# The start of a two-layer conditional residual kernel rewritten: loads on two queues, a shorter sort, and eight multiplications by zeros on TensorE

## The chip, the cores and the metric

The kernel runs on one core of a Trainium2 chip. The metric is the device time of one execution in microseconds (us). A profile is one further execution, recorded by the hardware profiler. Engines are named as the profile names them: PE is TensorE's matmul, PEld its weight load, DVE is VectorE, ACT is ScalarE, POOL is GpSimd, SP is the engine that only issues transfers. "SPq" and "ACTq" are the two engines' issuing of DMA transfers.

## What is computed

The input `x` is 128 batches of 64 channels by 512. Each batch `b` has a subject (0 to 7) and an adapter (0 to 6).

```
x  = x + einsum('bct,bcd->bdt', x, weights[subject]) + bias[subject][:, :, None]
H  = einsum('btd,od->bto', x, W)                       # W is 512 x 512
xa = einsum('btd,brd->btr', x, A[adapter])             # rank 16
x  = x + H + einsum('btr,bor->bto', xa, Bm[adapter]) * scalings[adapter]
```

Everything is fp32.

## The kernel before, in words

**Sorting.** Batches are sorted by adapter on the chip, so that two batches with the same adapter form a pair; a pair fills 128 partitions (two times 64 channels). 64 pairs are then processed in sorted order. The sort is made of two small matmuls that count adapters (L657, L658: `counts` and `earlier`), a chain of small DVE operations (L415 to L462), and three matmuls that turn `place` into tables (L680, L682). It gives three things: `order`, the adapters in the order in which they come (semaphore `order_ready`), `batch`, the sorted batch numbers (`batches_ready`), and `table` with subjects and adapter places (`others_ready`).

**Merged weights.** For each adapter in that order the kernel makes one matrix, W transposed plus the adapter's product, in four chunks of 128 by 512 (`m_product` L692, one matmul a chunk), kept as a high and a low part for fp32r matmuls: `m_add` (DVE) adds the product in PSUM to the transposed weight `wt`, `m_round` (ACT) makes `m_hi`, `m_split` (DVE) makes `m_lo`. The operands `a_parts` and `b_parts` are made the same way: the load `a_f` and the transposed `b_dup` (`turn_b`, four transposes L674) are each rounded by ACT and split by DVE. W arrives in `w_nat` (printed as o_ring, whose memory it shares) and is turned by TensorE in column blocks, `turn_w(c)` L664, and copied out by ACT, `copy_wt`.

**Pairs.** `layer0(j)` is 32 small matmuls (L716) on the pair's slot of `x_ring` (four slots) with `p_pair`, which POOL places with `bias_pair`. `x1_add` (DVE), `x1_round` (ACT), `x1_split` (DVE) follow, then `layer1(j)`, 12 matmuls of 128 by 512 (L739), then `copy_out` (ACT) and two stores. In the steady part TensorE does four `layer0` in a row every four pairs.

**Order by hand.** Every engine's program is written out; only semaphores tie them. SP issues, in order: the adapter numbers, `b_nat`, `p_all` twice, W blocks 0 and 1; then it waits for `order_ready` and issues `load_a(0)`, W block 2, the bias, W block 3; then it waits for `batches_ready` and issues eight loads of x (four pairs, `x_first`), `load_a(1)`, and `load_quad(4)`: the loads of pairs 4 to 7, each of which waits until `layer0` has freed its slot, in slot order 0, 2, 1, 3. ACT issues the scalings (spread over 128 partitions) and the subjects. On TensorE, before the first `layer1`, stand `layer0(0)`, `layer0(1)` and `turn_b(1)`; `layer0(2)` and `layer0(3)` stand between `layer1(0)` and `layer1(1)`, and `layer0` of pairs 4, 6, 5, 7 between `layer1(1)` and `layer1(2)`.

Of the kernel before, what the change touches and what calls it, by code (L numbers as in the profile page):

```python
# [33 lines left out]
def cond_residual_layers(nc, x, subject, bias, adapter, w, W, A, Bm, scal, out):  # L34
# [25 lines left out]
    with ExitStack() as ctx:  # L60
# [34 lines left out]
        scal_all = sb("scal_all", [P, K])  # L95
        neg = sb("neg", [P, 2])
# [4 lines left out]
        ids = sb("ids", [P, 2])  # L101
        vals = sb("vals", [P, 3], BF16)
        onehot = sb("onehot", [P, K], BF16)
        cnt_i = sb("cnt_i", [P, 2, K], I32)
        even_odd = sb("even_odd", [P, 2, K])
        key = sb("key", [P, K])
        prec = sb("prec", [P, K, K])
        prec_n = sb("prec_n", [P, 2, K, K])
        at_place = sb("at_place", [P, K, K])
        start = sb("start", [P, 2, K])  # L110
        last = sb("last", [P, K])
        quant = sb("quant", [P, 3, K])
        quant_b = sb("quant_b", [P, 3])
        small = sb("small", [P, 2])
# [5 lines left out]
        order_f = sb("order_f", [1, K])  # L120
# [4 lines left out]
        b_turned_at = ps[:, 4, :].rearrange("p (c n) -> p n c", c=TC)  # L125
# [19 lines left out]
        scal_in = sem("scal_in")  # L145
        consts = sem("consts")
# [5 lines left out]
        place_ready = sem("place_ready")  # L152
        batches_tabled = sem("batches_tabled")
# [6 lines left out]
        b_nat_ready = sem("b_nat_ready")  # L160
# [70 lines left out]
        def _(sp):  # L231
            with nc.allow_non_contiguous_dma(reason="indices, one per partition"):
                sp.dma_start(ids_i[:, 0:1], adapter.rearrange("(b a) -> b a", a=1)).then_inc(ids_in, 16)
            sp.dma_start(b_nat[:], Bm.rearrange("k (p c) r -> p k (c r)", c=TC)).then_inc(bnat_in, 16)
            for half in range(2):
                sp.dma_start(p_all[C * half:C * half + C], w.rearrange("s c d -> c s d")).then_inc(w0_in, 16)

            def load_w(c):

                cols = slice(c * P, c * P + P)  # L240
                sp.dma_start(w_nat[:, :, cols], W[:, cols].rearrange("(o p) t -> p o t", p=P)).then_inc(w_in[c], 16)

            load_w(0)
            load_w(1)
# [24 lines left out]
            load_w(2)  # L269
            sp.dma_start(bias_all[:], bias.rearrange("s d -> (s d)").rearrange("(a n) -> a n", a=1)  # L270
                         .to_broadcast([P, S * C]).rearrange("p (s d) -> p s d", s=S)).then_inc(bias_in, 16)
            load_w(3)
# [26 lines left out]
        def _(pool):  # L299
# [31 lines left out]
            pool.wait_ge(scal_in, 16)  # L331
            nc.gpsimd.tensor_tensor(b_nat[:], b_nat[:], scal_all[:].unsqueeze(2).to_broadcast([P, K, TC * R]),
                                    ALU.mult).then_inc(b_nat_ready, 1)
            pool.wait_ge(b_nat_ready, 1)
            regs = [pool.alloc_register(f"pool_word{i}") for i in range(2)]

            def dup_b(i):
                k, = words(pool, regs[:1], order[0:1, ds(i, 1)], K - 1)

                at_least(pool, b_turned, i)  # L340
                nc.gpsimd.tensor_copy(b_dup[:, :, 0:G, :], b_nat[:, ds(k, 1), :].rearrange("p k (c r) -> p (k c) r", c=TC)  # L341
                                      .unsqueeze(2).to_broadcast([P, TC, G, R])).then_inc(b_dupped, 1)
# [41 lines left out]
        def _(dve):  # L384
# [11 lines left out]
            def tt(o, a, b, op):  # L396
# [3 lines left out]
            over_k = [P, K, K]  # L400

            dve.wait_ge(consts, 2)
            iota_done = did(nc.vector.tensor_copy(iota[:], iota_i[:]))

# [6 lines left out]
            need(did(nc.vector.tensor_copy(ids[:, 0:1], ids_i[:, 0:1])))  # L411
            nc.vector.tensor_scalar(onehot[:], iota[:, 0:K], ids[:, 0:1], None, ALU.is_equal).then_inc(oh_ready, 1)
# [4 lines left out]
            cnt_done = did(nc.vector.tensor_copy(cnt_i[:, 0], counts))  # L417
            need(key_done)
            prec_done = tt(prec[:], key[:].unsqueeze(1).to_broadcast(over_k), key[:].unsqueeze(2).to_broadcast(over_k),
                           ALU.is_gt)  # L420
            need(cnt_done)
            odd_done = did(nc.vector.tensor_scalar(cnt_i[:, 1], cnt_i[:, 0], 1, None, ALU.bitwise_and))
            need(prec_done)
            place_of_done = did(nc.vector.tensor_reduce(quant[:, 1, :], prec[:], AX_X, ALU.add))
            need(odd_done)
            did(nc.vector.tensor_copy(even_odd[:, 1], cnt_i[:, 1]))
            even_done = tt(even_odd[:, 0], counts, cnt_i[:, 1], ALU.subtract)

            need(place_of_done)
            at_done = tt(at_place[:], quant[:, 1, :].unsqueeze(1).to_broadcast(over_k),  # L430
                         iota[:, 0:K].unsqueeze(2).to_broadcast(over_k), ALU.is_equal)
            need(even_done)

            prec_n_done = [tt(prec_n[:, h], prec[:], even_odd[:, h].unsqueeze(1).to_broadcast(over_k), ALU.mult)
                           for h in range(2)][-1]
            need(at_done)
            at_done = tt(at_place[:], at_place[:], iota[:, 0:K].unsqueeze(1).to_broadcast(over_k), ALU.mult)
            need(prec_n_done)
            start_done = did(nc.vector.tensor_reduce(start[:].rearrange("p h k -> p (h k)"),
                                                     prec_n[:].rearrange("p h k m -> p (h k) m"), AX_X, ALU.add))  # L440
            need(at_done)
            order_done = did(nc.vector.tensor_reduce(order_f[:], at_place[0:1], AX_X, ALU.add))
            need(start_done)

            tt(quant[:, 0, :], start[:, 0], earlier, ALU.add)
            left_done = tt(start[:, 1], start[:, 1], start[:, 0], ALU.subtract)
            need(order_done)
            nc.vector.tensor_copy(order[:], order_f[:]).then_inc(order_ready, 1)
            whole_done = did(nc.vector.tensor_reduce(small[:, 0:1], even_odd[:, 0], AX_X, ALU.add))
            last_done = tt(last[:], even_odd[:, 0], earlier, ALU.is_equal)  # L450
            did(nc.vector.tensor_copy(vals[:, 0:1], pid_i[:]))
            need(whole_done)
            need(did(nc.vector.scalar_tensor_tensor(out=start[:, 1], in0=start[:, 1], scalar=small[:, 0:1],
                                                    in1=even_odd[:, 0], op0=ALU.add, op1=ALU.subtract)))
            need(tt(quant[:, 2, :], last[:], start[:, 1], ALU.mult))

            need(tt(quant[:], quant[:], onehot[:].unsqueeze(1).to_broadcast([P, 3, K]), ALU.mult))
            dve.wait_ge(subject_in, 16)
            did(nc.vector.tensor_copy(vals[:, 1:2], ids_i[:, 1:2]))
            need(did(nc.vector.tensor_reduce(quant_b[:], quant[:], AX_X, ALU.add)))  # L460
# [19 lines left out]
            def m_add(t, chunk):  # L480

                dve.wait_ge(m_summed, t + 1)
                if isinstance(t, int) and t < TC:
                    dve.wait_ge(wt_copied, t + 1)
# [26 lines left out]
            b_split(0)  # L511
            a_split(0)
            m_add(0, 0)
            m_add(1, 1)
            m_split(0, 0)
            m_split(1, 1)
            m_add(2, 2)
# [301 lines left out]
```

## Time and profile before

| | us |
|---|---|
| median of three runs | 262.65 (261.12 to 262.7) |
| the profiled execution | 263.65 |
| its span, first to last instruction | 261.6 |
| PE busy | 237.2 (91%) |
| DVE, ACT, POOL busy | 142.9, 112.5, 75.9 |
| mean granted TensorE clock | 0.984 |

The profiled execution takes 2.05 us more than its span. The profile gives busy times, a line of the granted clock in 40 slices (each 6.54 us), the chain of waits that ended last, and groups of instructions; the timeline gives each instruction's start and duration.

### The profile page before, as it was taken

The numbers are of one execution on the slowest core, as the hardware profiler recorded it, in microseconds if no ns is written. First come the engines' busy times: TensorE is split into PE (matmuls) and PEld (weight loads), VectorE is DVE, ScalarE is ACT, GpSimd is POOL, SyncE is SP. The second block draws the span as 40 slices with busy tenths as digits, with TensorE's granted clock in tenths as the row PEclk, the third lists the DMA queues.
The fourth block names the chain that finished last, engine by engine and source line by source line (L and its number), as shares of the span: only waits on it lengthen the run. The fifth ranks groups of instructions, "written<-read, shape, count | busy, mean of one in ns | idle before, by whom it ended". The sixth has DMA issues, their size and how long they took to land.

```text
span 261.6 us, 9840 instructions
## 1 busy us (share of the span) xinstructions
PE 237.2 (91%) x2929; PEld 195.0 (75%) x2930; DVE 142.9 (55%) x242; ACT 112.5 (43%) x189; POOL 75.9 (29%) x284
## 2 busy tenths in 40 slices
PE   0487498999999999999999999999999998999993
PEld 0465386788887888788878887888878886888882
DVE  5669436747476564747474647556574744343300
ACT  2164405535354436444353535353634443343511
POOL 6346520045103530154005510355342423000000
PEclk9999859999999999999999999999999999999998
DMA  6582535255554656365536465456547362642331
GB/s 114 152 197 63 164 106 178 61 159 153 164 167 127 180 145 196 86 199 135 180 100 191 139 165 165 119 169 160 175 101 210 104 198 76 201 125 78 83 76 45
DMA packets 25825, 36.68 MB, mean 140 GB/s; under 512 B 6736, under 2 KB 8784, under 8 KB 25808
## 3 DMA queue, kind: packets, MB, share of 16 engines
q1 hardware_dynamic: 20400, 28.06, 39.8%
q10 hardware_dynamic: 5408, 8.40, 11.0%
q8 instruction: 10, 0.16, 0.3%
q14 instruction: 7, 0.06, 0.1%
HBM read 19.67 MB, written 16.78 MB: 139 GB/s over the span
## 4 chain that ended last, share of the span: by engine, by line
PE 84%; DMA 4%; DVE 4%; issue 3%; ACT 2%; SPq 1%; ACTq 0%
PE ps L739 68%; PE ps L716 13%; PE ps L692 3%; DMA a_f<-in_L_cond_A_dram 2%; SPq L256 1%; DVE m_f L486 1%; PE ps L674 1%; DMA x_ring<-in_x_dram 1%; DMA ids_i<-in_itok_B_dram 1%; ACT x_hi L576 1%; DVE m_lo L492 1%; DVE prec_n L397 0%; ACTq L602 0%; PE ps L664 0%; DVE x_lo L506 0%
## 5 line engine op out<-in xcount | busy, mean ns | idle before, releaser
L739 PE MATMUL ps<-m_hi,x_hi 128*128 x264 | 105.9, 401 | 3.0 <-DVE x_lo L506 1.8
L739 PE MATMUL ps<-m_hi,x_lo 128*128 x264 | 103.2, 391 | 0.0
L739 PE MATMUL ps<-m_lo,x_hi 128*128 x264 | 103.2, 391 | 0.0
L506 DVE TENSOR_TENSOR x_lo<-x,x_hi 128x512 fp32r<-128x512 f32 x64 | 44.5, 695 | 81.6 <-ACT x_hi L576 81.5
L368 POOL COPY p_pair<-p_all 64x64 f32 x128 | 41.8, 327 | 102.5 <-issue 54.8
L576 ACT ACTIVATE x_hi<-x 128x512 fp32r<-128x512 f32 x64 | 40.4, 632 | 50.0 <-DVE x L498 31.9
L585 ACT ACTIVATE o_ring<-ps 128x512 f32<-128x512 f32 x60 | 35.8, 596 | 60.3 <-PE ps L739 60.1
L739 PEld LDWEIGHTS ps<-m_hi,x_hi 128*128 128x128 f32 x264 | 49.8, 189 | 14.5 <-issue 3.6
L739 PEld LDWEIGHTS ps<-m_hi,x_lo 128*128 128x128 f32 x264 | 49.7, 188 | 10.8
L739 PEld LDWEIGHTS ps<-m_lo,x_hi 128*128 128x128 f32 x264 | 49.9, 189 | 9.7
L498 DVE TENSOR_TENSOR x<-ps,bias_pair 128x512 f32<-128x512 f32 x64 | 43.7, 683 | 10.7 <-PE ps L716 10.7
L716 PEld LDWEIGHTS ps<-p_pair,x_ring 64*64 64x64 f32 x2048 | 33.3, 140 | 11.8 <-issue 11.7
L716 PE MATMUL ps<-p_pair,x_ring 64*64 64x64 f32 x2048 | 35.6, 225 | 5.4 <-DMA x_ring<-in_x_dram 3.3
L379 POOL COPY bias_pair<-bias_all 128x64 f32 x128 | 28.4, 248 | 2.7 <-DMA bias_all<-in_fside_8xS_dram 2.4
L570 ACT ACTIVATE m_hi<-m_f 128x512 f32 (+1 forms) x32 | 20.1, 631 | 16.0 <-DVE m_f L486 16.0
L486 DVE TENSOR_TENSOR m_f<-ps,wt 128x512 f32<-128x512 f32 x32 | 21.8, 688 | 5.6 <-PE ps L692 4.0
L492 DVE TENSOR_TENSOR m_lo<-m_f,m_hi 128x512 f32 (+1 forms) x32 | 22.6, 705 | 0.7 <-ACT m_hi L570 0.5
L341 POOL COPY b_dup<-b_nat 128x256 f32 x8 | 3.6, 445 | 36.4 <-PE ps L674 34.6
L692 PE MATMUL ps<-b_parts,a_parts 128*128 128x512 f32 x32 | 12.8, 416 | 1.0 <-DVE a_parts L471 1.0
L692 PEld LDWEIGHTS ps<-b_parts,a_parts 128*128 128x128 f32 x32 | 6.2, 202 | 2.6 <-DVE a_parts L471 1.4
L477 DVE SCALAR_TENSOR_TENSOR b_parts<-b_parts,neg,ps 128x512 fp32r<-128x512 f32 x8 | 5.9, 735 | 1.7 <-ACT b_parts L565 1.7
L587 ACT ACTIVATE o_ring<-ps 64x512 f32<-64x512 f32 x4 | 2.4, 591 | 9.3 <-PE ps L739 9.3
(79 smaller groups left out, 57.1 us busy)
## 6 DMA issues: line engine op xcount, KB each, us to landing
x_ring<-in_x_dram SPq DMA_DIRECT2D x128, 128.0 KB, 2.7
out_dram<-o_ring ACTq DMA_DIRECT2D x64, 128.0 KB, 2.4
out_dram<-o_ring SPq DMA_DIRECT2D x64, 128.0 KB, 2.3
o_ring<-in_L_cond_W_dram SPq DMA_DIRECT2D x4, 256.0 KB, 4.5
a_f<-in_L_cond_A_dram SPq DMA_DIRECT2D x8, 128.0 KB
b_nat<-in_L_cond_Bm_dram SPq DMA_DIRECT2D x1, 256.0 KB, 4.2
p_all<-in_L_cond_weights_dram SPq DMA_DIRECT2D x2, 128.0 KB, 4.3
bias_all<-in_fside_8xS_dram SPq DMA_DIRECT2D x1, 256.0 KB, 5.3
```

Of the source, the lines that this page charges most:

```text
L368: nc.gpsimd.tensor_copy(p_pair[rows, slot, :], p_all[rows, ds(s[half], 1), :] .rearrange("p s d -> p (s d)")).then_inc(pair_ready, 1)
L379: nc.gpsimd.tensor_copy(bias_pair[:, slot, C * half:C * half + C], bias_all[:, ds(s[half], 1), :] .rearrange("p s d -> p (s d)")).then_inc ...
L486: nc.vector.tensor_tensor(m_f[:, chunk % 2], ps[:, 4 + chunk % 2, :], wt[:, chunk, :], ALU.add).then_inc(m_added, 1)
L492: nc.vector.tensor_tensor(m_lo[:, cols], m_f[:, chunk % 2], m_hi[:, cols], ALU.subtract).then_inc(m_ready, 1)
L498: nc.vector.tensor_tensor(x1[:, u % 2].rearrange("p c (h d) -> p c h d", h=2), l0_out(u).rearrange("p h (c d) -> p c h d", c=TC), bias_pai ...
L506: nc.vector.tensor_tensor(x1_lo[:, u % HELD], x1[:, u % 2], x1_hi[:, u % HELD], ALU.subtract).then_inc(x1_lo_ready, 1)
L570: nc.scalar.activation(m_hi[:, cols], m_f[:, chunk % 2], ACT.Copy).then_inc(m_hi_ready, 1)
L576: nc.scalar.activation(x1_hi[:, u % HELD], x1[:, u % 2], ACT.Copy).then_inc(x1_hi_ready, 1)
L585: nc.scalar.activation(o_ring[:, u % OR, :], ps[:, 2 + u % 2, :], ACT.Copy).then_inc(out_ready, 1)
L692: nc.tensor.matmul(ps[:, 4 + chunk % 2, :], a_parts[:, chunk * P:chunk * P + P], b_parts[:], start=True, stop=True).then_inc(m_summed, 1)
L716: mm = nc.tensor.matmul(x1_t[side * C:side * C + C, half, c * C:c * C + C], x_ring[rows, slot, at:at + C], p_pair[rows, u % PR, :], start= ...
L739: mm = nc.tensor.matmul(ps[:, bank, :], part[:, u % HELD, c, :], m[:, ds(k * (TC * T) + c * T, T)], start=(c == 0 and part is x1_hi and m ...
```

## The change

It does six things, nearly all before the first `layer1`.

1. **Loads.** SP issues the adapter numbers, W row blocks 0 and 1 (whole rows of 2 KB, where columns of 512 B were loaded), the subjects and one row of scalings (`scal_row`, 32 B). ACT issues `b_nat`, W row blocks 2 and 3, `p_all` twice and the bias. After `order_ready` SP issues only `load_a(0)`.
2. **Scalings.** A matmul of ones with `scal_row` spreads them; ACT copies them to `scal_all`. POOL no longer multiplies all of `b_nat`; each `dup_b` is a multiplication of its 128 by 256 block instead of a copy.
3. **Sort.** Most DVE steps work on 128 by 8 with an accumulated output in place of 128 by 64. `order` comes from a new matmul of `vals` with `firsts`, copied out by ACT, in place of a DVE reduction.
4. **Zeros.** TensorE multiplies `b_parts`, set to zero by a DVE memset, by itself (128 by 512, bf16): five times at its start, three times between the scalings' matmul and the order's.
5. **First merged matrix.** W is turned by row block into four PSUM banks, copied from there (two chunks by ACT, two by DVE), and the products of the first adapter are accumulated onto it in PSUM, so that `m_round_first` and `m_split_first` read PSUM and the first four `m_add` are gone.
6. **First pairs.** `layer0` of pairs 0 to 3 all stand before `layer1(0)`, `turn_b(1)` before `layer1(1)`, and the first `load_quad` takes its slots in the order 0, 1, 2, 3.

The core of the diff, engine by engine. On SP:

```diff
+            for o in range(2):
+                sp.dma_start(w_nat[:, o, :], W[o * P:o * P + P, :]).then_inc(w_in[o], 16)
+            with nc.allow_non_contiguous_dma(reason="indices, one per partition"):
+                sp.dma_start(ids_i[:, 1:2], subject.rearrange("(b a) -> b a", a=1)).then_inc(subject_in, 16)
+            sp.dma_start(scal_row[:], scal.rearrange("(a k) -> a k", a=1)).then_inc(scal_in, 16)
...
-                for i in (0, 2, 1, 3):
-                    sp.wait_ge(l0_done, i + 1 if isinstance(j, int) and j == XR else j - XR + (1, 3, 2, 4)[i])
+                first = isinstance(j, int) and j == XR
+                for i in range(L0_QUAD) if first else (0, 2, 1, 3):
+                    sp.wait_ge(l0_done, i + 1 if first else j - XR + (1, 3, 2, 4)[i])
...
             sp.wait_ge(order_ready, 1)
             load_a(0)
-            load_w(2)
-            sp.dma_start(bias_all[:], bias.rearrange("s d -> (s d)").rearrange("(a n) -> a n", a=1)
...
-            load_w(3)
```

On DVE:

```diff
+            nc.vector.memset(b_parts[:].bitcast(F32), 0.0).then_inc(zeroed, 1)
...
+            nc.vector.scalar_tensor_tensor(out=firsts[:], in0=iota[:, 0:K], scalar=place_of,
+                                           in1=was_first.to_broadcast([P, K]),
+                                           op0=ALU.is_equal, op1=ALU.mult).then_inc(firsts_ready, 1)
...
+            copy_wt(2)
+            copy_wt(3)
+            m_split_first(0)
             x1_add(0, 0)
-            m_split(2, 2)
+            m_split_first(1)
+            x1_add(1, 1)
             x1_split(0, 0)
```

On ACT:

```diff
+            act.wait_ge(scal_spread, 1)
+            nc.scalar.activation(scal_all[:], ps[:, 6, 0:K], ACT.Copy).then_inc(scal_ready, 1)
...
+            act.wait_ge(order_summed, 1)
+            nc.scalar.activation(order[:], ps[0:1, 7, 0:K], ACT.Copy).then_inc(order_ready, 1)
```

On TensorE:

```diff
+            pe.wait_ge(zeroed, 1)
+            keep_busy(5)
...
             nc.tensor.matmul(ps[:, 0, K:2 * K], before_b[:], onehot[:], start=True, stop=True).then_inc(counted, 1)
...
+            pe.wait_ge(scal_in, 16)
+            nc.tensor.matmul(ps[:, 6, 0:K], ones[0:1, :], scal_row[:], start=True, stop=True).then_inc(scal_spread, 1)
...
+            keep_busy(3)
+            pe.wait_ge(firsts_ready, 1)
+            nc.tensor.matmul(ps[0:1, 7, 0:K], vals[:, 3:4], firsts[:], start=True, stop=True).then_inc(order_summed, 1)
+            turn_w(0)
             pe.wait_ge(place_ready, 1)
```

How the rows on TensorE stand from its start to the products of the first adapter. Before (a row is the line, the operation, output and inputs, the shape, and what it waits for):

```order
L657 MATMUL ps<-onehot,ones_b 128x8 [waits oh_ready,consts_b]
L658 MATMUL ps<-onehot,before_b 128x8
L680 MATMUL ps<-place,vals 1x128 [waits place_ready]
L682 MATMUL ps<-place,vals 1x128 x2
L674 MATMUL ps<-ident,b_dup 128x128 [waits b_dupped]
L674 MATMUL ps<-ident,b_dup 128x128 x3
L664 MATMUL ps<-ident,o_ring 128x128 [waits w_in0]
```

The same place on TensorE after the change, where ps<-b_parts are the zeros, ps<-firsts the order and ps<-place the tables:

```order
L684 MATMUL ps<-b_parts 128x512 [waits zeroed]
L684 MATMUL ps<-b_parts 128x512 x4
L692 MATMUL ps<-onehot,ones_b 128x8 [waits oh_ready,consts,consts_b]
L693 MATMUL ps<-onehot,before_b 128x8
L695 MATMUL ps<-scal_row,ones 128x8 [waits scal_in]
L684 MATMUL ps<-b_parts 128x512 x3
L721 MATMUL ps<-firsts,vals 1x8 [waits firsts_ready]
L701 MATMUL ps<-ident,o_ring 128x128 [waits w_in0]
L701 MATMUL ps<-ident,o_ring 128x128 x3
L724 MATMUL ps<-place,vals 1x128 [waits place_ready]
L727 MATMUL ps<-place,vals 1x128 [waits order_ready]
```

Between the counts and the tables now stand the wait for the scalings' transfer, three multiplications of zeros, the order's matmul and the turning of one row block of W.

TensorE from the first pair's `layer0` to the first `layer1` (L739 before). Before:

```order
L716 MATMUL ps<-p_pair,x_ring 64x64 [waits pair_ready,x_first0,others_ready]
L716 MATMUL ps<-p_pair,x_ring 64x64 x15
L716 MATMUL ps<-p_pair,x_ring 64x64 [waits pair_ready,x_first1]
L716 MATMUL ps<-p_pair,x_ring 64x64 x15
L674 MATMUL ps<-ident,b_dup 128x128 [waits m_added,b_dupped]
L674 MATMUL ps<-ident,b_dup 128x128 x3
L221 TENSOR_LOAD table
L739 ISA [waits m_ready,x1_lo_ready]
```

And after the change, where `layer1` is L794:

```order
L773 MATMUL ps<-p_pair,x_ring 64x64 [waits pair_ready,x_first0]
L773 MATMUL ps<-p_pair,x_ring 64x64 x15
L743 MATMUL ps<-b_parts,a_parts 128x512 [waits wt_copied_too]
L773 MATMUL ps<-p_pair,x_ring 64x64 [waits pair_ready,x_first1,others_ready]
L773 MATMUL ps<-p_pair,x_ring 64x64 x15
L773 MATMUL ps<-p_pair,x_ring 64x64 [waits x1_ready,pair_ready,x_first2]
L773 MATMUL ps<-p_pair,x_ring 64x64 x15
L773 MATMUL ps<-p_pair,x_ring 64x64 [waits x1_ready,pair_ready,x_first3]
L773 MATMUL ps<-p_pair,x_ring 64x64 x15
L228 TENSOR_LOAD table
L794 ISA [waits m_ready,x1_lo_ready]
```

The third and fourth pair's `layer0` and their waits for x moved ahead of the first `layer1`, and `turn_b(1)` moved behind it.

## Rows read from the trace of the kernel before

**Rows 1.** The page: the granted clock in 40 slices, in tenths.

```profile
PEclk9999859999999999999999999999999999999998
```

**Rows 2.** Windows, PE: stretch, length, PE busy (instructions), granted clock, DMA share, GB/s.

```profile
60.00:240.00 180.00, 177.05 (x2324) 1.00 0.53 150
```

**Rows 3.** Timeline, the sort: start, duration, engine, line, operation, [idle before <-releaser].

```profile
4.53 0.17 PE L657 MATMUL ps<-onehot,ones_b 128*128 128x8 bf16 x1 [4.53 <-DVE onehot L412]
...
5.64 1.20 DVE L397 TENSOR_TENSOR prec_n<-prec,even_odd 128x64 f32<-128x64 f32 x2
...
7.36 0.15 DVE L448 CAST order<-order_f 1x8 int32<-1x8 f32 x1
...
8.24 0.70 SPq L251 DMA_DIRECT2D a_f<-in_L_cond_A_dram  x1
...
10.35 0.28 DVE L466 CAST batch<-ps 1x128 int32<-1x128 f32 x1 [0.36 <-PE ps L680]
...
11.81 2.54 SPq L256 DMA_DIRECT2D x_ring<-in_x_dram  x4
```

**Rows 4.** DMA issues: what, by whom, how many, size, median us to landing.

```profile
x_ring<-in_x_dram SPq DMA_DIRECT2D x128, 128.0 KB, 2.7
...
o_ring<-in_L_cond_W_dram SPq DMA_DIRECT2D x4, 256.0 KB, 4.5
...
b_nat<-in_L_cond_Bm_dram SPq DMA_DIRECT2D x1, 256.0 KB, 4.2
...
ids_i<-in_itok_B_dram ACTq DMA_DIRECT2D x1, 0.5 KB, 3.3
```

**Rows 5.** Chain of work that ended last, in order of time: start, duration, what.

```profile
8.24 4.79 DMA a_f<-in_L_cond_A_dram
...
21.97 3.02 PE ps L739 x12
...
29.32 2.77 DMA x_ring<-in_x_dram
...
32.57 3.69 PE ps L716 x128
36.27 3.84 PE ps L739 x12
```

**Rows 6.** Timeline, from the turning of B to the first m_f.

```profile
10.46 1.11 PE L674 MATMUL ps<-ident,b_dup 128*128 128x128 f32 x4
...
13.06 0.63 ACT L559 ACTIVATE a_parts<-a_f 64x512 fp32r<-64x512 f32 x1 [0.85 <-DMA a_f<-in_L_cond_A_dram]
...
13.72 0.74 DVE L471 SCALAR_TENSOR_TENSOR a_parts<-a_parts,neg,a_f 64x512 fp32r<-64x512 f32 x1 [0.66 <-ACT a_parts L559]
...
15.35 1.29 DVE L486 TENSOR_TENSOR m_f<-ps,wt 128x512 f32<-128x512 f32 x2 [0.89 <-PE ps L692]
...
19.51 0.66 PE L674 MATMUL ps<-ident,b_dup 128*128 128x128 f32 x4
```

**Rows 7.** Waits: who for whom, us in total, times, longest.

```profile
SPq L256 <- PE ps L716: 4.9, 1, 4.9
```

**Rows 8.** Windows of layer0 (L716) alone: PE busy, PEld busy, granted clock, DMA, GB/s.

```profile
32.00:37.00 5.00, 3.69 (x128) 3.54 (x128) 0.50 0.39 97
50.00:54.00 4.00, 2.10 (x128) 1.99 (x128) 1.00 0.43 108
```

**Rows 9.** Windows of layer1 (L739) alone, same columns.

```profile
26.00:28.85 2.85, 2.83 (x12) 2.17 (x12) 1.00 0.42 109
```

**Rows 10.** Windows, all engines: PE, PEld, DVE, ACT, POOL busy, granted clock, DMA, GB/s.

```profile
28.90:32.50 3.60, 0.36 (x2) 0.00 (x0) 1.29 (x2) 1.40 (x3) 2.00 (x11) 0.84 0.71 212
30.90:37.70 6.80, 5.13 (x132) 4.75 (x133) 1.99 (x3) 0.81 (x2) 2.45 (x12) 0.53 0.38 99
```

**Rows 11.** The page's groups: POOL's copies for the pairs | busy, mean ns | idle before.

```profile
L368 POOL COPY p_pair<-p_all 64x64 f32 x128 | 41.8, 327 | 102.5 <-issue 54.8
...
L379 POOL COPY bias_pair<-bias_all 128x64 f32 x128 | 28.4, 248 | 2.7 <-DMA bias_all<-in_fside_8xS_dram 2.4
```

More of the change, by code:

```diff
@@ L100, in cond_residual_layers @@
         ids_i = sb("ids_i", [P, 2], I32)
-        ids = sb("ids", [P, 2])
-        vals = sb("vals", [P, 3], BF16)
+        vals = sb("vals", [P, 4], BF16)
+        firsts = sb("firsts", [P, K], BF16)
         onehot = sb("onehot", [P, K], BF16)
         cnt_i = sb("cnt_i", [P, 2, K], I32)
-        even_odd = sb("even_odd", [P, 2, K])
+        even = sb("even", [P, K])
         key = sb("key", [P, K])
[L107 to L114, printed above, removed]
+        picked = sb("picked", [P, 4, K])
+        own = sb("own", [P, 12])
         place = sb("place", [P, B], BF16)
@@ L436, in _ @@
[L436 to L457, printed above, removed]
+            need(own_done)
+            place_done = did(nc.vector.tensor_scalar(picked[:, 2], key[:], own_key, None, ALU.is_gt, ALU.add,
+                                                     accum_out=place_of))
@@ L465, in _ @@
+            nc.vector.tensor_scalar(place[:], iota[:], at, None, ALU.is_equal).then_inc(place_ready, 1)
             dve.wait_ge(batches_tabled, 1)
@@ L653, in _, with keep_busy @@
         def _(pe):
+            zeros = b_parts[:].bitcast(BF16)
+            def keep_busy(times):
+                for _ in range(times):
+                    nc.tensor.matmul(ps[:, 3, :], zeros[:, 0:P], zeros[:, 0:T], start=True, stop=True)
+            pe.wait_ge(zeroed, 1)
+            keep_busy(5)
             pe.wait_ge(consts_b, 3)
+            pe.wait_ge(consts, 3)
             pe.wait_ge(oh_ready, 1)
@@ L685, in _, with m_product_first @@
             turn_b(0)
-            turn_w(0)
-            turn_w(1)
+            for o in range(1, TC):
+                turn_w(o)
+            for c in range(TC):
+                nc.tensor.matmul(ps[:, FIRST + c, c * P:c * P + P], ident_b[:], ident_b[:],
+                                 start=False, stop=True).then_inc(wt_turned, 1)
+            def m_product_first(chunk):
+                if chunk < 2:
+                    pe.wait_ge(wt_copied, chunk + 1)
+                else:
+                    pe.wait_ge(wt_copied_too, chunk - 1)
+                nc.tensor.matmul(ps[:, FIRST + chunk, :], a_parts[:, chunk * P:chunk * P + P], b_parts[:],
+                                 start=False, stop=True, skip_group_check=True).then_inc(m_summed, 1)
             def m_product(t, chunk):
-                at_least(pe, m_added, t - 1)
+                at_least(pe, m_added, t - TC - 1)
                 nc.tensor.matmul(ps[:, 4 + chunk % 2, :], a_parts[:, chunk * P:chunk * P + P], b_parts[:],
@@ L748, in _ @@
             pe.wait_ge(b_ready, 1)
[L749 to L755 removed]
+            m_product_first(0)
+            m_product_first(1)
+            m_product_first(2)
             first_inputs(0)
             layer0(0, 0)
[L758 to L760 removed]
+            m_product_first(3)
+            pe.wait_ge(others_ready, 2)
+            for j in range(1, L0_QUAD):
+                first_inputs(j)
+                layer0(j, j)
             regs = [pe.alloc_register(f"pe_word{i}") for i in range(2)]
@@ L775, in step @@
                     turn_b(n + 2)
+                if n is None and j == 1:
+                    turn_b(1)
                 if n is not None and u == HEAD + 2:
```

202 lines of the change are left out of this document (109 added, 93 removed).

## The prediction, made before the changed kernel ran

> **What bounds the kernel now.** I read the page first, then windows, then the chain in order of time, then the timeline of the first 40 us. The page's line of the granted clock dips in the fifth and sixth slice [rows 1]. From 60 to 240 us PE is busy 177.05 of 180 us [rows 2]: there TensorE is the bound, and what is done before it starts moves the end one for one. The change leaves the steady part as it is, so the question is only how early the steady part begins.
>
> The chain of the start has four pieces to keep in mind. The load of A is issued at 8.24 us and takes 4.79 us to land, the first `layer1` starts at 21.97 us, a load of x is waited for until 32.1 us, and then `layer0` and `layer1` of the next pairs take 3.69 and 3.84 us [rows 5]. The load of x is late because its issue is: SP waited 4.9 us for a `layer0` [rows 7]. That is `layer0(2)`, which stands behind `layer1(0)`, and the loads for pairs 5 to 7 stand behind that wait. PE is then nearly idle from 28.9 to 32.5 us (0.36 us busy of 3.6), and the granted clock is 0.53 over 30.9 to 37.7 us [rows 10], that is the 1.2 GHz level for nearly all of that stretch.
>
> The page shows a granted clock of full speed at the very start, but the instructions say otherwise: four transposes take 1.11 us at 10.46 us and 0.66 us at 19.51 us [rows 6]. I read TensorE as at its lower level until about 17 us.
>
> **The change part by part.**
>
> *When the order is ready.* Before, counts are out at 4.7 us and `order` is copied by DVE at 7.36 to 7.51 us [rows 3]. DVE's new chain is shorter: of about 19 small steps up to `order` the two `prec_n` alone took 1.20 us [rows 3] and are gone; about ten steps of some 0.12 us remain, so `firsts` is ready near 6.0 us. But the order now also needs TensorE, which first waits for the scalings. Their transfer is SP's fifth. I put its issue near 2.7 us, from four issues of about 0.46 us ahead of it after 0.85 us. Its landing is bounded from below by the 3.3 us of a transfer of 0.5 KB that had its queue almost to itself, and from above by the 4.5 us of a W block that stood behind others [rows 4]: 6.0 to 7.2 us. I take 6.0, by the row of its own size. Then come its matmul (0.2 us), three multiplications of zeros, the order's matmul (0.2) and ACT's copy (0.27). One 128 by 512 matmul takes 2.83/12 = 0.24 us at 2.4 GHz [rows 9], so three take 0.7 us, or 1.4 at the lower level. That gives 7.4 to 8.1 us; I take 8.0, so 0.5 us later than now. The load of A is issued 0.73 us after the order, at 8.75 us.
>
> A rule bears on this wait. The trace shows that the 0.5 KB of subjects landed in 3.3 us while `b_nat`, issued at nearly the same time on the other queue, took 4.2 us [rows 4]: the small transfer was not held by the large one. The Trainium skill (DMA: Bandwidth & Descriptors, "Queues, rings and completion order") says that a transfer's semaphore increment lands only after every earlier write of that DMA engine, across its queues. By the page the scalings would be held by W's first two blocks and `b_nat` too, and the order would be ready near 9.2 us, 1.2 us later than I take; this case is a rival below, by the 4.5 us row.
>
> *The load of A.* It no longer shares its queue with W blocks 2 and 3 and the bias. A load of x of the same 128 KB takes 2.7 us [rows 4], so it lands at 11.5 us, where it was 13.03. ACT's rounding and DVE's split take 0.63 and 0.74 us [rows 6]: `a_parts` is ready at 12.9 us, where it was 14.46.
>
> *From A to the first `layer1` on DVE.* After `a_parts` DVE has two copies of W, then two splits, two `x1_add` and one `x1_split`: seven operations of 128 by 512, which run at one each 0.62 us when nothing is waited for (two in 1.29 us, rows 6 show it). So `x1_lo` of pair 0 is ready at 12.9 + 7 x 0.63 = 17.3 us. The two remaining splits of M end before `layer1(0)` reaches its third and fourth chunk.
>
> *The first four x loads.* All four `layer0` now stand ahead of `layer1(0)`. TensorE turns one block of W after the order (1.06 us at the low level, as four transposes of 1.11 us [rows 6] show), then makes the batch table. So `batch` is copied near 9.4 us, where it was 10.35 to 10.63 [rows 3]. SP's first x load follows 1.2 us later (11.81 after 10.63 [rows 3]), at 10.7 us. Four issues take 2.54 us [rows 3], so the eighth starts at 15.2 and lands 2.7 us later, at 17.9 us. `layer0(3)` takes 2.10/4 = 0.5 us [rows 8], and `layer1(0)` starts at 18.4 us. That is later than DVE's 17.3, so **this path decides: 21.97 - 18.4 = 3.6 us gained.** DVE's `place`, some ten small steps behind `firsts`, is ready near 7.3 us and hidden behind the order's wait.
>
> *From there to the second group of pairs.* Now it is 32.57 - 21.97 = 10.6 us. After: two `layer1` of 2.83 us [rows 9], `turn_b(1)` 0.66 [rows 6], one product 0.24, together 6.55 us, to 24.95 us. The x loads for it: SP has issued the first eight by 15.8, `load_a(1)` by 16.5, and eight more from 17.0; the last starts at 21.5 and lands at 24.2 to 24.5 us, just hidden by `layer1(1)`. If that cover is gone, each 0.1 us of lateness costs 0.1. **Gained: 10.6 - 6.55 = 4.05 us.**
>
> *The lower level of the clock.* `layer0` of four pairs took 3.69 us at it and takes 2.10 at full clock [rows 8]; the 12 matmuls behind took 3.84 [rows 5] against 2.83 [rows 9]. If the idle stretch is gone I expect the low stretch gone: **1.6 + 1.0 = 2.6 us.**
>
> *Costed at nothing.* The five zeros need 5 x 0.48 = 2.4 us at the low level and run while TensorE waits for the one-hot at 4.53 us [rows 3]. DVE's memset runs while it waits for iota. The multiplication in `dup_b` is off the path: POOL has slack. A pair takes it two copies of 0.33 us and two of 0.25 [rows 11], 1.15 us and, with the gaps between, some 1.5; eight pairs from 10.4 us end near 22.5 us, ahead of the 24.95 where they are needed. If that cover is gone, POOL's lateness adds to the start of the second group one for one.
>
> Sum: 3.6 + 4.05 + 2.6 = 10.2 us. Against the profiled execution of 263.65 us that is 253.4; the median of the runs shown is 1.0 us lower, so I expect 252.4 us.
>
> **The rivals.**
>
> *A, the clock falls anyway (25%, 255 us).* Between 12.9 and 18.4 us TensorE has only three products and four `layer0`, some 3 us of work in 5.5, waiting on x. Before, a stretch with 0.36 us of work in 3.6 was followed by 6.8 us at the lower level [rows 10], which cost 2.6 us. If the same comes here, over `layer1(0)`, most of the third term is given back: 252.4 + 2.6 = 255.0. Against it: the stretch is fuller than the one that brought the fall, and the zeros keep the engine active early. The Trainium skill (TensorE: Matmul & The Clock Gate, Part 1) says the low clock is the default, sustained activity releases it and idleness brings it back; it would have the zeros work and the gaps behind them undo it.
>
> *B, the scalings are late (15%, 253.6 us).* They land at 7.2 instead of 6.0 us, the bound of [rows 4]; order, batch and A all slip by 1.2 us.
>
> *C, better (15%, 250.8 us).* The zeros bring 2.4 GHz before 6 us: three zeros save 0.7 us, the block of W 0.4 us, and A and x come 1.1 us earlier; x loads closer to 2.4 us give the rest.
>
> *D, x still waited for (5%, 257 us).* If the second eight loads of x or POOL's pairs land 4 to 5 us later than worked out, the 3.6 us stall and with it the low clock return, and only the first term and a little are left: 259 us at worst.
>
> *E, slower (2%, above 264 us).* The lower level lasts. Four `layer0` cost 1.6 us more and 12 matmuls 1.0 us more at it, so each `layer1` at the low level loses about 1 us of 3.8. To eat 10.2 us it must hold over the first ten pairs, nearly 40 us. The longest low stretch before PE's last work is 6.8 us [rows 10]; nothing speaks for it but that the start has more waits.
>
> *F, the zeros do nothing.* The first stretch stays at 1.2 GHz until about 17 us as before. My sum already has the low level there, so the time is that of the forecast; they cost nothing either.
>
> **How the numbers follow.** The forecast as worked out has 38%, with F in it. A, B, C, D and E have 25, 15, 15, 5 and 2%. A and B together would give 256.2; C at its best 249.5. The range 249.5 to 256.3 leaves out D, E and tails of A and C, together under 2 in 10. About 1% is what a measurement can tell from no change, here 2.6 us. Faster by over 1% (under 260.0): 0.95; within 1%: 0.03; slower: 0.02.
>
> **What would show it.** `layer1(0)` starts near 18.4 us and waits last for x or for `layer0(3)`; the wait of 4.9 us on SP is gone; the second group's `layer0` starts near 25 us; the granted clock has no low stretch in the slices after the first; four transposes of B take 0.66 us if C is right and 1.1 if not; the scalings' matmul is near 6.0 us. Wrong would be: a low clock over the first `layer1` (A), the order's matmul above 8.5 us (B), PE waiting for DMA before the second group (D).

## The result: no gain, where 4% was forecast

The changed kernel took 264.6 us (median of 20 runs, 263.47 to 266.49); the kernel before, in 20 runs, 263.27 us (261.12 to 266.44). The ratio is 1.0066, with a 95% interval of 1.004 to 1.0091: slower by 0.7%. I had forecast 252.4 us. The trace below is of an execution of 266.09 us, at a mean granted clock of 0.971; the 20 runs had 0.971 to 0.994, and the five from 0.993 up took 263.5 to 264.6 us, so the stretches of low clock that the trace shows were shorter in some executions.

The profile after. The page's span and granted clock in 40 slices:

```profile
span 264.4 us, 9858 instructions
...
PEclk9977959999999999999999999999999999999998
```

The span is 2.8 us longer than before, and the clock line has two dips where [rows 1] has one. The chain that ended last, in order of time (start, duration, what):

```profile
2.74 5.18 DMA scal_row<-in_L_cond_scalings_dram
...
8.55 1.39 PE ps L684 x3
...
10.96 4.97 DMA a_f<-in_L_cond_A_dram
...
24.02 3.03 PE ps L794 x12
...
30.47 5.00 issue
35.46 3.69 PE ps L773 x128
39.16 3.67 PE ps L794 x12
...
47.82 5.48 PE ps L794 x24
```

Against [rows 5]: the first `layer1` starts at 24.02 us, where it was 21.97 and I had put 18.4; A takes 4.97 us to land, where I had put 2.7; and there is again an idle stretch, 5.00 us long, before the second group's `layer0`, which starts at 35.46 us instead of the 24.95 I expected. Behind it `layer0` takes 3.69 us, the same number as in [rows 5]: the low clock came back with the stall. The steady part starts 2.7 us late (the last line; before, a like block started at 45.11 us), and the span grew by 2.8.

SP's timeline (start, duration, engine, line, what), and POOL's waits (who, for whom, us in total, times, longest):

```profile
20.97 5.12 SPq L257 DMA_DIRECT2D x_ring<-in_x_dram  x8
```

```profile
POOL b_dup L336 <- PE ps L714: 7.0, 1, 7.0
POOL b_dup L336 <- ACT order L635: 6.7, 1, 6.7
```

The loads of x are not what is late: SP issued the second group's eight without a pause from 20.97 to 26.1 us, and a load of x took 2.4 to 3.0 us to land, so the last was in by 29.1 us, ahead of the stall. The first POOL line names what I had missed (the second is `dup_b(0)`, which waits for the order). POOL's timeline around it, and TensorE's transposes that it waits for:

```profile
20.30 0.41 POOL L377 COPY bias_pair<-bias_all 128x64 f32 x2
...
27.70 0.61 POOL L336 TENSOR_TENSOR b_dup<-b_nat,scal_all 128x256 f32 x1 [6.99 <-PE ps L714]
...
29.30 0.30 POOL L366 COPY p_pair<-p_all 64x64 f32 x1 [0.99 <-POOL b_dup L336]
...
34.50 0.41 POOL L377 COPY bias_pair<-bias_all 128x64 f32 x2
```

```profile
26.89 0.60 PE L714 MATMUL ps<-ident,b_dup 128*128 128x128 f32 x4
```

POOL has placed pairs 0 to 3 by 20.7 us. Next in its program is `dup_b` of the third adapter, ahead of pair 4. It may not overwrite `b_dup` until `turn_b(1)` has read it, and the change moved `turn_b(1)` from before `layer1(0)` (19.51 us, [rows 6]) to behind it (ending at 27.5 us). Pairs 4 to 7 are placed only then, from 29.30 to 34.91 us (the last POOL line is pair 7's), and TensorE's `layer0` of the group, which needs all four, starts at 35.46 us. The page calls TensorE's 5.00 us "issue", since it waits on a count that POOL raised piece by piece.

### The profile page after: what moved, and what is told of

It is laid out like the page before. It is cut to its first block, busy times and chain, and to the rows that moved or that the text cites. A ratio compares the mean times of both kernels' runs of the same rounds, so it can differ in the third digit from the quotient of the medians.

```text
span 264.4 us, 9858 instructions
## 1 busy us (share of the span) xinstructions
PE 242.2 (92%) x2940; PEld 196.9 (74%) x2941; DVE 138.8 (53%) x242; ACT 111.5 (42%) x189; POOL 75.5 (29%) x283
## 4 chain that ended last, share of the span: by engine, by line
PE 86%; issue 4%; DMA 4%; DVE 2%; ACT 1%; SPq 1%; ACTq 0%
PE ps L794 68%; PE ps L773 13%; PE ps L749 2%; DMA scal_row<-in_L_cond_scalings_dram 2%; DMA a_f<-in_L_cond_A_dram 2%; PE ps L714 1%; PE ps L743 1%; DVE m_f L484 1%; DVE m_lo L490 1%; PE ps L684 1%; ACT x_hi L600 0%; ACTq L626 0%; SPq L242 0%; DVE a_parts L471 0%; DVE x L508 0%
## 5 line engine op out<-in xcount | busy, mean ns | idle before, releaser
L794 PE MATMUL ps<-m_hi,x_hi 128*128 x264 | 105.7, 400 | 1.3 <-DVE m_lo L490 1.2
L794 PE MATMUL ps<-m_hi,x_lo 128*128 x264 | 103.3, 391 | 0.0
L794 PE MATMUL ps<-m_lo,x_hi 128*128 x264 | 103.1, 391 | 0.0
L794 PEld LDWEIGHTS ps<-m_hi,x_hi 128*128 128x128 f32 x264 | 49.8, 189 | 12.8 <-issue 1.9
L794 PEld LDWEIGHTS ps<-m_hi,x_lo 128*128 128x128 f32 x264 | 49.7, 188 | 10.7
L794 PEld LDWEIGHTS ps<-m_lo,x_hi 128*128 128x128 f32 x264 | 49.8, 189 | 9.7
L773 PEld LDWEIGHTS ps<-p_pair,x_ring 64*64 64x64 f32 x2048 | 34.8, 145 | 14.1 <-issue 14.1
L773 PE MATMUL ps<-p_pair,x_ring 64*64 64x64 f32 x2048 | 37.1, 231 | 7.2 <-issue 7.2
L594 ACT ACTIVATE m_hi<-m_f 128x512 f32 (+1 forms) x28 | 17.7, 632 | 13.1 <-DVE m_f L484 13.1
L484 DVE TENSOR_TENSOR m_f<-ps,wt 128x512 f32<-128x512 f32 x28 | 19.2, 690 | 5.4 <-PE ps L749 3.8
L490 DVE TENSOR_TENSOR m_lo<-m_f,m_hi 128x512 f32 (+1 forms) x28 | 19.7, 703 | 0.1
L336 POOL TENSOR_TENSOR b_dup<-b_nat,scal_all 128x256 f32 x8 | 5.2, 652 | 44.6 <-PE ps L714 37.6
L749 PE MATMUL ps<-b_parts,a_parts 128*128 128x512 f32 x28 | 10.7, 389 | 0.0
L471 DVE SCALAR_TENSOR_TENSOR a_parts<-a_parts,neg,a_f 64x512 fp32r<-64x512 f32 x8 | 5.9, 738 | 2.2 <-ACT a_parts L576 2.2
L714 PE MATMUL ps<-ident,b_dup 128*128 128x128 f32 x32 | 5.4, 294 | 1.2 <-DVE m_f L484 0.9
```

What stands on the lines that cost most here:

```text
L484: nc.vector.tensor_tensor(m_f[:, chunk % 2], ps[:, 4 + chunk % 2, :], wt[:, chunk, :], ALU.add).then_inc(m_added, 1)
L490: nc.vector.tensor_tensor(m_lo[:, cols], m_f[:, chunk % 2], m_hi[:, cols], ALU.subtract).then_inc(m_ready, 1)
L594: nc.scalar.activation(m_hi[:, cols], m_f[:, chunk % 2], ACT.Copy).then_inc(m_hi_ready, 1)
L749: nc.tensor.matmul(ps[:, 4 + chunk % 2, :], a_parts[:, chunk * P:chunk * P + P], b_parts[:], start=True, stop=True).then_inc(m_summed, 1)
L773: mm = nc.tensor.matmul(x1_t[side * C:side * C + C, half, c * C:c * C + C], x_ring[rows, slot, at:at + C], p_pair[rows, u % PR, :], start= ...
L794: mm = nc.tensor.matmul(ps[:, bank, :], part[:, u % HELD, c, :], m[:, ds(k * (TC * T) + c * T, T)], start=(c == 0 and part is x1_hi and m ...
```

## The experiments

All times below stand against runs of the kernel before on the same chip (263.04, 263.04, 263.08 and 262.87 us in the four groups).

### POOL's order

`pool_dup_later`, one edit of the changed kernel:

```diff
-                place_at = n + 2 if n is not None and u == HEAD else 1 if n is None and j == 1 else None
+                place_at = n + 2 if n is not None and u == 0 else 1 if n is None and j == 1 else None
```

> The changed kernel with one edit: POOL makes each later dup_b (those of the third adapter on) after it has placed the pairs of the group, not before. Theory P (POOL's dup_b of the third adapter waits for turn_b(1), which the change moved behind layer1(0); pairs 4 to 7 are placed only after it, so TensorE idles 5.0 us from 30.5 to 35.5 us and its clock falls): the idle 5.0 us and most of the low clock behind it (3.69 for 2.10 us of layer0, some 1 us of layer1) go, the time falls by 6 to 7.6 us against the changed kernel, to 257 to 258.5 us. Rival X (the loads of x for pairs 4 to 7 are what is waited for, as I forecast could happen): the time stays within 1 us of 264.6.

Measured: 258.26 us, ratio 0.9842 (0.9774 to 0.991), below the changed kernel by 6.3 us in the medians and 5.9 in the ratios. Its chain:

```profile
23.10 3.01 PE ps L794 x12
...
26.55 2.77 PE ps L794 x12
...
29.55 2.02 PE ps L773 x128
```

The stall is gone and `layer0` takes 2.02 us. Theory P is shown; theory X falls. One line of POOL's program, which the change had left as it was, had turned a gain of 1.6% into a loss, because TensorE's `turn_b(1)` had moved.

### The part of the change by itself

`before_layer0_ahead` is the kernel before with `layer0(2)` and `layer0(3)` moved ahead of `layer1(0)` and the first `load_quad` in the order 0 to 3:

```diff
             layer0(1, 1)
             turn_b(1)
+            for j in range(2, L0_QUAD):
+                first_inputs(j)
+                layer0(j, j)
```

> The kernel before with one part of the change alone: layer0 of pairs 2 and 3 ahead of layer1(0), the first load_quad in the order 0 to 3; turn_b(1) stays ahead of both. My prediction's second and third term by themselves: layer1(0) starts about 1 us later (23 us, layer0(3) waits for x1_add(1)), the wait for x at 29 to 32.6 us goes, so the second group's layer0 starts near 29 us instead of 32.57, and the low clock (2.6 us) goes: 263 - 3.5 - 2.6 = 257 us. Rival: if POOL's pairs or the loads still come late, 261 us or more.

Measured: 258.84 us, ratio 0.9845 (0.9788 to 0.9902). Its chain:

```profile
23.27 5.75 PE ps L738 x24
...
29.24 0.82 issue
30.06 2.09 PE ps L717 x128
```

The wait for x and the low clock over the second group are gone. So my second and third term were real. From `layer1(0)` to the second group it is 6.8 us, where it was 10.6 (3.8 us gained, 4.05 forecast), and `layer0` and `layer1` behind take 2.09 and 2.94 us, where they took 3.69 and 3.84 (2.5 gained, 2.6 forecast). Against that, `layer1(0)` starts 1.3 us later (23.27 against 21.97). That leaves 5.0 us, as in the spans (256.6 against 261.6); the medians differ by 4.2. With its own `turn_b(1)` in place, POOL does not stall here. Moving `layer0` thus gives 1.6% alone; all the other edits of the change together, with POOL's order mended, give nothing beyond it (0.9842 against 0.9845).

### The small transfers and the zeros

`small_first` issues the scalings and the subjects ahead of W's two blocks on SP.

```diff
+            sp.dma_start(scal_row[:], scal.rearrange("(a k) -> a k", a=1)).then_inc(scal_in, 16)
             with nc.allow_non_contiguous_dma(reason="indices, one per partition"):
                 sp.dma_start(ids_i[:, 1:2], subject.rearrange("(b a) -> b a", a=1)).then_inc(subject_in, 16)
+            for o in range(2):
+                sp.dma_start(w_nat[:, o, :], W[o * P:o * P + P, :]).then_inc(w_in[o], 16)
-            sp.dma_start(scal_row[:], scal.rearrange("(a k) -> a k", a=1)).then_inc(scal_in, 16)
```

> The changed kernel with one edit: on SP the scalings and the subjects are issued ahead of the two row blocks of W. Theory S (the 32 B of scalings land 5.2 us after their issue because they stand behind W's blocks on SP's queue): they land near 1.33 + 3 = 4.3 us instead of 7.9, the order comes near 6.4 us instead of 10.25, layer1(0) starts about 3 us earlier than 24.0. But the stall by POOL stays, whose chain (turn_b(1), dup_b, four pairs placed) starts from layer1(0), so the gain is 3 to 3.8 us: 261 us. Rival L (small transfers take 5 us whenever large ones of either queue are in flight): the order stays near 10 us and the time at 264.6.

Measured: 263.62 us, ratio 1.0019 (0.998 to 1.0057). Its timeline:

```profile
4.08 0.59 PE L695 MATMUL ps<-scal_row,ones 1*128 1x8 f32 x2
...
6.56 0.15 ACT L635 ACTIVATE order<-ps 1x8 int32<-1x8 f32 x1
...
8.68 1.12 PE L701 MATMUL ps<-ident,o_ring 128*128 128x128 f32 x4 [2.51 <-DMA o_ring<-in_L_cond_W_dram]
```

Theory S holds for the order: 6.56 us instead of 10.08. But the time fell by about 1 us (the intervals of the two ratios meet), not by 3 to 3.8: TensorE now waits 2.51 us for W's first block, which stands ahead of the tables, so the batch numbers come at 10.0 us, and the pairs' placing is late. And the clock takes part of the gain. The window in which TensorE waits for the pairs (columns as below, under `fill_the_wait`), and `layer1(0)` on the chain:

```profile
17.00:20.00 3.00, 1.39 (x64) 1.17 (x64) 2.40 (x5) 1.75 (x3) 1.57 (x9) 1.00 0.32 87
```

```profile
21.79 3.99 PE ps L794 x12
```

`layer1(0)` starts 2.2 us earlier than in the changed kernel, but takes 3.99 us instead of 3.03: after 3 us with 1.39 of work the granted clock is 0.50 from 20.5 to 23.8 us. That is my rival A as I had put it.

`no_zeros` leaves out both calls of `keep_busy`.

> The changed kernel without its eight multiplications of zeros. Theory N (the zeros raise no clock, and the three ahead of the order stand on the chain for 1.4 us): order 1.4 us earlier, time 1 to 1.5 us lower, 263.3 us, and the granted clock of the first 13 us unchanged at the lower level. Rival W (the zeros do keep the clock up for part of the start): the time rises by 1 us or more.

Measured: 263.18 us, ratio 1.0031 (0.9995 to 1.0067); the order is out at 8.61 us, 1.47 earlier. That is 1.4 us below the changed kernel by the medians and 0.9 by the ratios, whose intervals meet, so the price on the end is likely and not shown. The batch numbers gain less than the order, 0.64 us (10.68 against 11.32): they also need the subjects, which took 7.1 us to land (issued at 2.26, behind W's two blocks). `pool_and_small` joins the first two edits, `pool_small_no_zeros` takes the zeros from that.

> The changed kernel with both edits: POOL's later dup_b behind the group's pairs, and the scalings and subjects ahead of W. If both theories hold and their gains add: 264.6 - 7 - 3.5 = 254 us. If the second group's x loads are now what is waited for, up to 1.5 us of that is lost, 255.5 us. If the x loads and not POOL bound it, 260 us or more.

> The changed kernel with POOL's dup_b later, the small transfers first, and none of the eight zeros. With the small transfers first, the three zeros end (6.07 us) near the moment firsts is ready, and W's first block, which lands near 8.6 us, holds the tables anyway. Theory N (zeros change nothing but the chain they stand on): the order comes some 0.4 us earlier, the time stays within 0.7 us of 257.65. Rival W (the zeros hold the clock): it rises by 1 us or more.

Measured: 257.65 us, ratio 0.9823 (0.9755 to 0.9892), and 257.49 us, ratio 0.977 (0.9705 to 0.9835). The gains did not add to 254: W's block and the pairs bind, as in `small_first`, and the clock falls over `layer1(0)` in both traces (3.94 and 5.41 us for its 12 matmuls). The zeros make no difference that can be told here.

`tables_first_no_zeros` moves `turn_w(0)` behind the tables and `turn_b(0)`.

```diff
-            turn_w(0)
             pe.wait_ge(place_ready, 1)
...
-            for o in range(1, TC):
+            for o in range(TC):
```

> As the last, and TensorE makes the tables before it turns W's first block. Theory T (in the last kernels the tables wait for W's block, 2.5 us): batch is copied near 7.3 us instead of 10.0, x loads start near 8.7 instead of 11.5, the pairs are placed 2 us earlier, and layer1(0) starts near 19 us instead of 21.2; time 255.3 us. Rival A (the load of A with its 5 us is now what decides): A lands at 12.3 us as now, layer1(0) near 20 us, time 256.5 us.

Measured: 255.69 us, ratio 0.9737 (0.9672 to 0.9802). The batch numbers come at 7.1 us, `layer1(0)` at 20.93, and what stands right ahead of it is `layer0(3)`, which waited for POOL's placing of pair 3. `layer1(0)` takes 3.02 us: here the clock did not fall, though TensorE had as little work ahead of it (1.31 us of the 3 from 17 to 20 us) as in `small_first`. What decides between the two, no run shows. Theory T's time is met, its start of `layer1(0)` is 2 us too early. `pairs_earlier` adds two edits for POOL: `dup_b(1)` after the first four pairs, and `p_all` issued ahead of W's blocks 2 and 3.

> tables_first_no_zeros with two edits for POOL: dup_b(1) after the first four pairs, and ACT issues p_all ahead of W's blocks 2 and 3. There layer1(0) starts at 20.93 us right behind layer0(3) (19.93), which waited for POOL's pair 3; DVE's x1_split(0) was done at 18.9. Theory: layer1(0) moves to DVE's 18.9 to 19.3 us, time 255.7 - 1.8 = 253.9 us. Rival: the loads of x for the second group (issued one by one behind x_first and load_a(1)) then bind, gain under 0.5 us.

Measured: 253.76 us, ratio 0.9653 (0.9604 to 0.9702). Its chain:

```profile
18.00 3.01 PE ps L794 x12
...
24.59 2.09 PE ps L773 x128
...
34.65 5.47 PE ps L794 x24
```

These are about the times that I had forecast for the change itself (18.4 and 24.95 us), but it took six edits more to get there, and A's load still takes 4.39 us, not the 2.7 forecast. It has the lowest median of the versions that compute the whole result, 3.5% below the kernel before; `pairs_earlier_zeros` and `all_together` below can't be told from it.

`pairs_earlier_zeros` puts the eight zeros back into it.

> pairs_earlier with the eight zeros put back in their places. Theory N: they stand on the order's chain for some 0.3 us (small transfers first, three zeros end near 6.0 us) and raise no clock: the granted clock reaches 2.4 GHz near 13 us as without them, time within 0.8 us of 253.76. Rival W: the clock comes up by 8 us, the transposes of B and W take 0.66 us in place of 1.1, and the time falls by over 0.5 us.

Measured: 254.39 us, ratio 0.9689 (0.9638 to 0.974). Its transposes of B behind the zeros, and the same four in `pairs_earlier` without zeros:

```profile
4.60 1.46 PE L687 MATMUL ps<-b_parts 128*128 128x512 bf16 x3
...
7.88 1.11 PE L717 MATMUL ps<-ident,b_dup 128*128 128x128 f32 x4 [0.59 <-POOL b_dup L336]
```

```profile
7.72 1.12 PE L716 MATMUL ps<-ident,b_dup 128*128 128x128 f32 x4 [0.42 <-POOL b_dup L336]
```

1.11 and 1.12 us are both the lower level (0.66 at the higher, [rows 6]). Five zeros in 2.3 us and three in 1.5 us raised nothing that reached the next work. Nor did they bring the higher level sooner: single transposes of W fall from 0.42 to 0.27 us each at 13.3 us in the changed kernel and 13.8 in `pool_dup_later`, with zeros, and at 14.0 in `no_zeros` and 12.9 in `pool_small_no_zeros`, without. Theory N holds, rival W falls: what the zeros are for does not happen.

### The clock during the wait for A

`fill_the_wait` is `pool_dup_later` with eight matmuls of constants where TensorE waits for `a_parts`:

```diff
+            pe.wait_ge(batches_ready, 1)
+            for _ in range(8):
+                nc.tensor.matmul(ps[:, 1, 0:256], ident_b[:], before[:].bitcast(BF16), start=True, stop=True)
             pe.wait_ge(a_ready, 1)
```

> pool_dup_later (258.26 us) with eight more matmuls of 128 by 256 (bf16, constants, result unused) where TensorE waits for a_parts after it has turned W (14.7 to 17.1 us). There the granted clock fell from 17.3 to 20.7 us. Theory H (it is that idle wait that brings the fall): the clock stays up, products and layer0 run at 0.7 in place of 1.1 us, but layer1(0) waits for DVE, so time falls by 0 to 0.5 us. Rival: the clock falls all the same, or later, over layer1(0), and the time rises by 1 us or more.

Measured: 258.89 us, ratio 0.9852 (0.9804 to 0.99). The stretch of the products and first `layer0` (window, length, busy of PE, PEld, DVE, ACT, POOL, granted clock, DMA, GB/s), in `pool_dup_later` and here:

```profile
17.20:20.70 3.50, 3.50 (x48) 2.17 (x52) 2.60 (x5) 1.68 (x5) 1.96 (x10) 0.51 0.68 170
```

```profile
17.20:20.70 3.50, 3.33 (x100) 2.41 (x100) 3.48 (x6) 2.62 (x6) 1.92 (x10) 1.00 0.60 164
```

The granted clock is 1.00 where it was 0.51, and TensorE does 100 instructions where it did 48. The mean granted clock of its four runs is 0.996 to 0.998, where `pool_dup_later` has 0.983 to 0.998. So a fill in the right gap does keep the clock up, and theory H holds; the gap that brought the fall is the one before the products. The end does not gain: `layer1(0)` still waits for DVE's chain (22.82 against 23.10 us), and later, at 31.27 us, TensorE stands idle for 1.27 us within the second group's `layer0`, for which the trace names no cause. The Trainium skill (TensorE: Matmul & The Clock Gate, Part 1) says that activity releases the low clock and idleness brings it back; this pair of runs agrees.

### The first load of A

> tables_first_no_zeros with one transfer more: SP loads adapter 0's A into the same tile once, and waits for it, before the order is ready. The first load of A takes 4.2 to 5.0 us in every kernel so far, 2 us more than a load of x of the same size. Theory C (it is the first touch of A that costs): the real load then lands in 2.7 to 3 us, a_parts is ready 1.5 to 2 us earlier, and the time is lower by up to 1.5 us. Rival D (it is this form of transfer, four times the same 16 rows, that is slow every time): it takes 4.2 us or more again, and the time stays or rises by 0.5 us by the added traffic.

`a_read_before` read A once ahead of time. Measured: 259.46 us, ratio 0.9867 (0.981 to 0.9924). The real load was issued at 11.79 us, since SP had to wait for the first, and was in at 16.3: 4.55 us again. Theory C falls. The loss against `tables_first_no_zeros` is 3.8 us, and the load is issued 4.7 us later there.

> tables_first_no_zeros with the first load of A as four transfers of 16 rows, two from SP and two from ACT, in place of one that reads 16 rows four times. The one transfer took 4.2 to 5.0 us in every kernel, also when A had been read before (4.55 us). Theory F (its form is slow): each of the four lands 2.6 us after its issue, A is in 3.3 us after the first, a_parts 1.2 to 2 us earlier. The pairs still bind (layer0(3) at 19.9), so the time stays within 0.5 us of 255.7. Rival G (what is slow is the load that comes after an idle stretch or beside the other loads, whatever its form): A lands 4.2 us or more after its issue again.

Measured: 257.79 us, ratio 0.9814 (0.9753 to 0.9874), by the medians 2.1 us worse than `tables_first_no_zeros`: the four parts, issued from 7.21 us on both queues, were in at 14.4. Theory F falls. `all_together`, this on top of `pairs_earlier`:

> pairs_earlier and a_in_four together. With the pairs out of the way A binds through DVE's chain: layer1(0) near 17.7 us, time 252.7 us. If the x loads of the second group bind, 253.9 us as pairs_earlier alone.

Measured: 254.07 us, ratio 0.9669 (0.9631 to 0.9707), no better than `pairs_earlier`; A was in 5.0 us after its issue.

> pairs_earlier with every load of A replaced by 64 whole rows of x, the same 128 KB at the same moment from the same queue (so the second layer's adapter part is computed from wrong numbers; only the time is read). Theory F2 (the form of A's load, 16 rows read four times, is slow): the first load lands 2.7 to 3 us after its issue instead of 4.4, a_parts is ready 1.4 us earlier, time lower by up to 1 us. Rival G (it is the moment, behind the transfers of W and p_all, that is slow): it lands 4 us or more after its issue and the time stays.

Measured: 253.66 us, ratio 0.9668 (0.9616 to 0.9719). The eight loads' time to landing, the first being the longest:

```profile
DMA to landing us min/median/max: 2.4/2.5/4.5
```

With whole rows of x in place of A the first load still takes 4.5 us (issued 6.90, waited for until 11.4) and the later ones 2.5. So at this place it is neither the tensor, nor its repeated rows, nor the first touch, but the moment. Two things mark that moment: the loads of the start run just ahead, and it is the first load of the program whose address comes from a register.

In the changed kernel itself, traffic of the earlier loads can't be the reason. Its windows right before and during the load of A, which was issued at 10.96 us (the last two columns are the DMA share and GB/s):

```profile
10.00:12.00 2.00, 1.72 (x9) 1.10 (x9) 0.28 (x1) 0.61 (x3) 0.90 (x2) 1.00 0.00 0
```

```profile
14.00:14.50 0.50, 0.50 (x9) 0.49 (x7) 0.37 (x1) 0.00 (x0) 0.34 (x2) 1.00 0.26 102
```

Nothing moved from 10 to 12 us, and from 14.0 to 14.5 the share was 0.26, which is 4.2 of the 16 DMA engines, although the first loads of x were issued from 13.20 us on. In `pairs_earlier`, where the issue fell among the loads of the start, the share from 7 to 9 us was 1.04. So the repeated rows are cleared only for the busy moment, where `a_as_x_rows` tried it; with the DMA engines idle no run replaced them. Which causes cost the 2 us, and whether they are the same in both places, stays open.

## Why the prediction was wrong, point by point

The sum, term by term: `layer1(0)` started at 24.02 us instead of 18.4 (5.6 us), from there to the second group it was 11.4 us instead of 6.55 (4.9), and `layer0` and `layer1` behind took 2.4 us more than at full clock. That is 12.9 us, for the 12.7 between the profiled execution and its forecast (266.09 against 253.4).

- **"The multiplication in `dup_b` is off the path: POOL has slack": the step that failed.** POOL's lateness was put at nothing: I had worked out its eight pairs as one unbroken run of 1.5 us each, from 10.4 to "near 22.5 us". They ran from 13.75 to 34.91 us, with 7.0 us of waiting inside. I had read TensorE's order around `turn_b(1)` and priced its 0.66 us, but did not ask who waits for it: POOL's next `dup_b`, with four pairs queued behind. It cost the second term (5.00 us idle) and the third (low clock) together; mended, 6.3 us come back. My rival D had named late pairs of POOL's as a possibility, with 5%, no cause, and 259 us at worst.
- **The start of `layer1(0)`: forecast 18.4, measured 24.02, and 23.10 with POOL mended.** This is the other half, 5.6 us: the first term was a gain of 3.6 us and became a loss of 2.05. I had named the x loads as what decides, and it was A, through DVE's chain, for which I had 17.3 us: the order was 2.2 us late, A's load 2.3 us longer, and from `a_parts` to `x1_lo` DVE took 5.9 us (17.36 to 23.27) for my 4.4, with waits between that I had left out. The two bullets below are the first two of these.
- **The scalings: bounded 6.0 to 7.2 us, measured 7.92.** 5.18 us from issue to landing, outside my upper bound of 4.5, because I took its own size for the nearest row and not its place behind two blocks of W. Issued first, it was in by 4.08 us. The Trainium skill (DMA: Bandwidth & Descriptors, "Queues, rings and completion order") has a completion wait for the DMA engine's earlier writes, in its other queues too; the order near 9.2 us that I had worked out beside it was nearer to the 10.25 measured than my 8.0. `small_first` agrees for SP's own queue; what ACT's queue adds, no run shows. Rival B was right in kind, too small in size.
- **The load of A: put at 2.7 us, measured 4.97.** The trace before had 4.79, which I laid to the W blocks queued behind it. As one transfer it took between 4.2 us (`no_zeros`) and 5.9 us (`tables_first_no_zeros`) in all of the kernels run.
- **The clock (rival A, 25%).** It fell in the changed kernel over the products and the first `layer0`, one stage earlier than I had put it, where filling the gap moved the end by nothing that can be told; and over `layer1(0)`, as I had put it, in `small_first`, `pool_and_small` and `pool_small_no_zeros`.
- **The second and third terms as mechanisms were right.** `before_layer0_ahead` shows them, 3.8 us of 4.05 and 2.5 of 2.6.
- **The zeros.** F was right that no clock is gained, and C's 2.4 GHz before 6 us did not come. F's "they cost nothing either" was wrong for three of them, which stood 1.39 us on the order's chain; the sum itself had them there, at 0.7 to 1.4 us.
- **Rival E (above 264 us, 2%)** gave about the number that came, but by a low clock over ten pairs, which did not happen: meeting its number would be luck.
- **What bounds the end** was right throughout: every gain at the start of the steady part reached the end one for one. From the block that starts at 45.11 us before, at 47.82 in the changed kernel and at 34.65 in `pairs_earlier`, it is 216.5 to 216.6 us to the end of the span in each.

## What to carry to other kernels

When an instruction is moved, ask who waits for it, on every engine, and what is queued behind that waiter; an engine with slack loses it at once when its next instruction is a wait in program order. A small transfer on which a chain hangs goes first in its queue, not behind bulk loads. Work that only keeps TensorE busy kept the clock up in the gap right before the work that wanted it, and raised nothing at the start; it can pay only where TensorE is what the end waits for, and no run here gained by it.

## What the hardware showed beyond that

The page's granted clock reads 1.00 from the start of each trace, while transposes at 8 to 12 us take 1.11 us for four, the time of the lower level; the durations have to be read beside it. 32 bytes took 5.18 us to land behind 512 KB on their queue, with 1.25 MB issued on the other by 4.6 us.
